# A decoder layer on one core: rows for the band mask, columns for the denominators, separate banks for maximum and exponential, and a pipeline of six steps over quads

## The reference

```
n = layernorm(x)
x = x + softmax(band(q k^T / sqrt(8))) v @ Wo      # self: query t sees keys t-63 .. t
n = layernorm(x)
x = x + softmax(q k^T / sqrt(8) - 100*mask) v @ Wo + bo   # cross: 77 tokens of ctx, with biases
n = layernorm(x); p = n shifted by one token
r = sigmoid((mu_r*n + (1-mu_r)*p) @ W_r^T); k = (mu_k*n + (1-mu_k)*p) @ W_k^T
x = x + r * (relu(k)^2 @ W_v^T)
```

## Time and profile before

| | |
|---|---|
| Runs | 1101.64 us (median of 3; 1100.23 to 1105.47) |
| Profiled execution | span 1103.0 us from first to last instruction; no other time of it is recorded |
| TensorE busy | 873.3 us (79%) |
| DVE, ACT, POOL busy | 681.8, 421.8, 194.1 us |
| Mean granted TensorE clock | 0.904 of full speed |
| DMA | 92.18 MB in 81317 packets; queue 1 busy 38.2% of 16 engines |

### The profile page before, as it was taken

One profiled execution on the slowest core, in us unless ns is written; L12 is line 12 of the kernel. 1 busy time (PEld: TensorE's weight loads), 2 busy tenths in 40 slices (PEclk: granted clock), 3 DMA queues, 4 the chain that ended last, 5 costly groups with the idle time before them and its releaser, 6 DMA issues.

```text
span 1103.0 us, 33918 instructions
## 1 busy us (share of the span) xinstructions
PE 873.3 (79%) x13841; PEld 613.2 (56%) x13967; DVE 681.8 (62%) x1540; ACT 421.8 (38%) x600; POOL 194.1 (18%) x176
## 2 busy tenths in 40 slices
...
GB/s 39 100 28 118 79 120 79 109 93 91 50 92 112 77 128 77 128 65 83 72 90 99 77 128 77 128 69 86 71 100 89 77 128 77 125 59 24 79 12 10
DMA packets 81317, 92.18 MB, mean 84 GB/s; under 512 B 14944, under 2 KB 75059, under 8 KB 76655
## 3 DMA queue, kind: packets, MB, share of 16 engines
q1 hardware_dynamic: 81262, 91.39, 38.2%
...
...
## 4 chain that ended last, share of the span: by engine, by line
PE 37%; DMA 26%; issue 12%; SPq 9%; ACT 7%; DVE 4%; POOL 4%; POOLq 0%; ACTq 0%; DVEq 0%
DMA q_stack<-q_scr 11%; DMA cq_stack<-cq_scr 9%; SPq L332 4%; PE score L975 4%; DMA q_scr<-q_parts 4%; PE score L1047 4%; PE sums L999 4%; PE score L971 4%; PE sums L1006 3%; PE score L986 3%; PE score L1063 2%; SPq L324 2%; PE score L1059 2%; ACT probs L539 2%; POOL cq_parts L455 2%
## 5 line engine op out<-in xcount | busy, mean ns | idle before, releaser
L548 ACT ACTIVATE cprobs<-score 77x1024 f32<-77x1024 f32 x128 | 129.6, 1013 | 234.6 <-PE score L1082 232.3
L539 ACT ACTIVATE probs<-score 128x1024 f32<-128x1024 f32 x128 | 129.4, 1023 | 135.8 <-PE score L1063 135.8
L813 DVE TENSOR_REDUCE cneg_max<-score 128x8 f32<-128x616 f32 x128 | 102.4, 800 | 77.8 <-PE score L1047 75.9
L798 DVE TENSOR_REDUCE neg_max<-score 128x8 f32<-128x1024 f32 x64 | 78.1, 1225 | 100.2 <-PE score L975 99.2
L971 PE MATMUL score<-band,pick_hi 128*128 128x512 bf16 x111 | 48.6, 520 | 61.3 <-DMA q_stack<-q_scr 59.5
L1047 PE MATMUL score<-ck_stack,cq_stack 99*128 99x77 bf16 x1024 | 60.7, 205 | 44.7 <-DMA cq_stack<-cq_scr 33.1
L1047 PEld LDWEIGHTS score<-ck_stack,cq_stack 99*128 99x128 bf16 x1024 | 47.0, 101 | 77.4 <-issue 34.6
L999 PE MATMUL sums<-cprobs,cv_heads 128*32 128x128 f32 x2048 | 82.9, 280 | 8.6 <-ACT cprobs L548 8.6
L447 POOL TENSOR_TENSOR rstd<-var_eps,neg_half 128x4 f32<-128x4 f32 x48 | 48.5, 1011 | 214.5 <-DVE var_eps L743 207.1
L1082 PE MATMUL score<-cq_stack,ck_stack 128*77 128x256 bf16 x512 | 78.2, 282 | 8.3 <-DMA cq_stack<-cmax_mid 8.3
L999 PE MATMUL sums<-probs,v_heads 128*32 128x128 f32 x2048 | 83.8, 282 | 0.0
...
## 6 DMA issues: line engine op xcount, KB each, us to landing
k_stack<-k_scr SPq DMA_DIRECT2D x32, 384.0 KB, 5.7
...
```

Source lines behind the costliest of these rows:

```text
L539: nc.scalar.activation(probs[:, k % 3].rearrange("p g a q -> p (g a q)"), score[ST_SLOT[k]][:, :], ACT.Exp).then_inc(exp_done, 1)
L548: nc.scalar.activation(cprobs[0:TC, k % 2].rearrange("p g a q -> p (g a q)"), score[k % 2][0:TC, :], ACT.Exp).then_inc(cexp_done, 1)
L813: nc.vector.tensor_reduce(cneg_max[:, a, :, b].rearrange("p (n i) -> p n i", n=2), src, AX_X, ALU.max, negate=True).then_inc(cmax_taken, 1)
```

## The change

All programs are rewritten. In parts:

1. **Stacks.** `q_stack` and `k_stack` hold one pair of sequences (p = 0 or 1) and one head in each column block: rows 0 to 63 are constants (an identity for the upper 64 queries, `key_mask` for the keys), rows 64 to 111 the 48 rows of parts, and 112, 113 the two maximum rows. Products for the upper queries use rows from 0 and get the band mask with them; those for the lower queries use rows from 64 and keep a mask product (`band_lo`, `band_loT`). `cq_stack` and `ck_stack` hold even pairs of heads in rows 0 to 52 and odd ones in rows 64 to 116, so a product spans half of the array's rows.
2. **Scores.** Turned self scores are computed without the quarter that the band hides: 16 products of 64 columns for the upper queries of one sequence, and 32 for the lower queries of two. There are 6 exponentials a quad for 8. Cross products are one head each.
3. **Denominators** are columns 16 and 17 of each head pair's 32 columns of `v_heads`, set to one. The sums are copied by ACT (`take_sums`), turned on TensorE (`turn_sums`), divided on DVE with tokens on partitions (`divide`), and turned back (`turn_att`): 24 more 128x128 turns a quad.
4. **Banks.** `score_max` serves only maxima and `score_exp` only exponentials, one tile of two banks each.
5. **Layer norms** go to POOL except for `bn_stats`: 9 small operations, a power, and two of 128x512. `x_step` replaces the two `mix_a`, `x1b` goes through DRAM and back, `x_res` is loaded again and not copied.
6. **Transfers** are by pair and by quad: 63 issues a quad. Parts are stored in pieces of 256 or 154 tokens.
7. **Pipeline.** `step(s)` works on quads s to s-5: 21 steps, of which s = 5 to 15 are full. q0: norm, q, k. q1: v, maxima, first half of the self attention. q2: second half, output, cross projections. q3: cross values, cross maxima, first half. q4: second half, output, norm. q5: feed forward.

The order on TensorE in a full step: last values of the first cross half (q4); `max_upper` q1; `scores_lower` q2; turns of q4; values q2; `max_upper`; `scores_upper` q2; feed forward products of q5 between `max_lower` q1 and more values; v of q1; four `cross_max` q3, three more and the first `cross_scores` of q4 with their values between them, with turns and projections of q2 and q0; then `scores_upper`, `scores_lower` q1; `max_upper`, `max_upper`, `max_lower` of q1's second pair, with projections of q2 and q4 between them; `cross_scores` and values of q3 between four `cross_max` of q3; turn of q4's norm; first `scores_upper` of q1's second pair.

```diff
-        q_stack = sb("q_stack", [P, 2, G, QB, T], BF16)
-        k_stack = sb("k_stack", [P, G, QB, T], BF16)
-        score = [stack.enter_context(nc.psum_tensor(f"score{n}", [P, 1024], F32)) for n in range(2)]
+        q_stack = sb("q_stack", [P, 2, 2, G, PB, T], BF16)
+        k_stack = sb("k_stack", [P, 2, 2, G, PB, T], BF16)
+        v_heads = sb("v_heads", [P, 2, QB, G, 32])
+        score_max = stack.enter_context(nc.psum_tensor("score_max", [P, 1024], F32))
+        score_exp = stack.enter_context(nc.psum_tensor("score_exp", [P, 1024], F32))
+        sums = [stack.enter_context(nc.psum_tensor(f"sums{n}", [P, PB, 2, T], F32)) for n in range(2)]
...
-                    for m in range(2):
-                        nc.tensor.matmul(dst[:, 512 * m:512 * m + 512], band[:, 0, :], ident_bf[:, :, :],
-                                         start=True, stop=False)
-                    for i in range(4):
-                        g = 2 * i + j
-                        last = nc.tensor.matmul(dst[:, 256 * i:256 * i + 256], k_stack[:, g, b, :],
-                                                q_stack[:, :, g, b, :], start=False, stop=(i % 2 == 1))
-                    last.then_inc(sT_made, 1)
...
+            def max_upper(q, p, b):
...
+                for g in range(G):
+                    for a in range(2):
+                        last = nc.tensor.matmul(score_max[HALF * a:HALF * a + HALF, T * g:T * g + T],
+                                                q_stack[0:ROW1, p, a, g, b, HALF:T], k_stack[0:ROW1, p, a, g, b, :],
+                                                start=True, stop=True)
+                last.then_inc(s_made, 1)
...
+            def max_lower(q, p):
+                for b in range(PB):
+                    nc.tensor.matmul(score_max[:, 512 * b:512 * b + 512], pick_lo[:, :, :], band_lo[:, :, :],
+                                     start=True, stop=False)
+                    for g in range(G):
+                        c = 512 * b + HALF * g
+                        for a in range(2):
+                            last = nc.tensor.matmul(score_max[HALF * a:HALF * a + HALF, c:c + HALF],
+                                                    q_stack[ROW0:ROW1, p, a, g, b, 0:HALF],
+                                                    k_stack[ROW0:ROW1, p, a, g, b, 0:HALF],
+                                                    start=False, stop=(g == G - 1))
+                last.then_inc(s_made, 1)
...
+            def scores_upper(q, p, b):
...
+                for a in range(2):
+                    for g in range(G):
+                        c = 512 * a + HALF * g
+                        last = nc.tensor.matmul(score_exp[:, c:c + HALF], k_stack[0:ROWS_SELF, p, a, g, b, :],
+                                                q_stack[0:ROWS_SELF, p, a, g, b, HALF:T], start=True, stop=True)
+                last.then_inc(sT_made, 1)
...
+            def scores_lower(q, p):
...
+                        for a in range(2):
+                            last = nc.tensor.matmul(score_exp[HALF * a:HALF * a + HALF, c:c + HALF],
+                                                    k_stack[ROW0:ROWS_SELF, p, a, g, b, 0:HALF],
+                                                    q_stack[ROW0:ROWS_SELF, p, a, g, b, 0:HALF],
+                                                    start=False, stop=(g == G - 1))
...
+            def upper(p, b, a, js=(0, 1)):
+                for j in js:
+                    for i in range(4):
+                        g = 2 * i + j
+                        c = 512 * a + HALF * g
+                        last = nc.tensor.matmul(sums[0][32 * i:32 * i + 32, b, a, HALF:T], v_heads[:, a, PB * p + b, g, :],
+                                                probs[:, 2 * b, c:c + HALF], start=(j == 0), stop=(j == 1),
+                                                tile_position=(0, 32 * i))
+                return last
...
+            def turn_four(dst, src):
+                for n in range(4):
+                    last = nc.tensor.transpose(dst[:, P * n:P * n + P], src(n), ident[:, :])
+                return last
+            def turn_sums(q, p, dst):
+                pe.wait_ge(raw_ready, 2 * q + p + 1)
+                turn_four(dst, lambda n: raw[:, n, :]).then_inc(raw_turned, 1)
...
+            def cross_max(q, p, b, a):
...
+                for i in range(4):
+                    for j in range(2):
+                        r, c = HALF * j, 512 * j + TC * i
+                        last = nc.tensor.matmul(score_max[:, c:c + TC], cq_stack[r:r + SHIFT_CROSS, p, i, a, b, :],
+                                                ck_stack[r:r + SHIFT_CROSS, p, i, a, b, :], start=True, stop=True)
+                last.then_inc(cs_made, 1)
...
+            def cross_scores(q, p, b, a):
...
+                for i in range(4):
+                    for j in range(2):
+                        r, c = HALF * j, 512 * j + T * i
+                        last = nc.tensor.matmul(score_exp[0:TC, c:c + T], ck_stack[r:r + ROWS_CROSS, p, i, a, b, :],
+                                                cq_stack[r:r + ROWS_CROSS, p, i, a, b, :], start=True, stop=True)
+                last.then_inc(csT_made, 1)
...
+            def divide(src, turned, inv, inv_ready, dst, ready, dst_turned, q, p):
...
+                heads = src[:, :].rearrange("p (n c) -> p n c", c=32)
+                nc.vector.reciprocal(inv[:, :, :], heads[:, :, 16:18]).then_inc(inv_ready, 1)
+                if later(q):
+                    dve.wait_ge(dst_turned, q)
+                dve.wait_ge(inv_ready, 2 * q + p + 1)
+                nc.vector.tensor_tensor(dst[:, p].rearrange("p b (n j d) -> p (b n) j d", j=2, d=DH),
+                                        heads[:, :, 0:16].rearrange("p n (j d) -> p n j d", j=2),
+                                        inv[:, :, :].unsqueeze(3).to_broadcast([P, 16, 2, DH]), ALU.mult)\
+                    .then_inc(ready, 1)
...
+            def moments_of(n, q):
+                pool.wait_ge(ln_stats[n], QB * q + QB)
+                if later(q):
+                    pool.wait_ge(ln_out[n], q)
+                mo, st = moments[n], stats[n]
+                nc.gpsimd.tensor_tensor(mo[:, 0], st[:, :, 1], st[:, :, 4], ALU.add).then_inc(ln_moments[n], 1)
+                nc.gpsimd.tensor_tensor(mo[:, 1], st[:, :, 1], st[:, :, 4], ALU.subtract).then_inc(ln_moments[n], 1)
+                nc.gpsimd.tensor_tensor(mo[:, 2], st[:, :, 2], st[:, :, 5], ALU.add).then_inc(ln_moments[n], 1)
+                pool.wait_ge(ln_moments[n], 7 * q + 3)
...
+                pool.wait_ge(ln_moments[n], 7 * q + 7)
+                nc.gpsimd.tensor_tensor(root[n][:, :], var_eps[n][:, :], neg_half[:, :], ALU.pow)\
+                    .then_inc(ln_root[n], 1)
+                pool.wait_ge(ln_root[n], q + 1)
+                nc.gpsimd.tensor_tensor(rstd[n][:, :], root[n][:, :], root[n][:, :], ALU.add).then_inc(ln_rstd[n], 1)
...
+            def norm_of(n, src, q, turned):
...
+                mean = moments[n][:, 3, :].unsqueeze(2).to_broadcast([P, QB, D])
+                nc.gpsimd.tensor_tensor(xn[n][:, :, :], src[:, :, :], mean, ALU.subtract).then_inc(ln_centred[n], 1)
+                pool.wait_ge(ln_rstd[n], q + 1)
+                pool.wait_ge(ln_centred[n], q + 1)
+                nc.gpsimd.tensor_tensor(xn[n][:, :, :], xn[n][:, :, :],
+                                        rstd[n][:, :].unsqueeze(2).to_broadcast([P, QB, D]), ALU.mult)\
+                    .then_inc(ln_out[n], 1)
...
+            def make_stack_rows():
+                dve.wait_ge(bands_made, 4)
+                nc.vector.tensor_copy(q_stack[0:HALF].rearrange("r p a g b t -> r (p a g b) t")[:, :, HALF:T],
+                                      ident[0:HALF, 0:HALF].unsqueeze(1).to_broadcast([HALF, 2 * H * PB, HALF]))\
+                    .then_inc(stack_rows, 1)
+                nc.vector.tensor_copy(k_stack[0:HALF].rearrange("r p a g b t -> r (p a g b) t"),
+                                      key_mask[:, :].unsqueeze(1).to_broadcast([HALF, 2 * H * PB, T]))\
+                    .then_inc(stack_rows, 1)
+                nc.vector.memset(k_stack[96:P].rearrange("r p a g b t -> r (p a g b t)"), 1.0)\
+                    .then_inc(stack_rows, 1)
...
+                for n, rows in enumerate((slice(32, 64), slice(96, 128))):
+                    nc.gpsimd.memset(cq_stack[rows].rearrange("r p i a b t -> r (p i a b t)"), 1.0)\
+                        .then_inc(cross_rows, 1)
+                    nc.gpsimd.memset(ck_stack[rows].rearrange("r p i a b t -> r (p i a b t)"), 1.0)\
+                        .then_inc(cross_rows, 1)
+                    pool.wait_ge(cross_rows, 2 * n + 2)
...
+            def store_self(parts, scr, lo, stored, q):
+                sp.wait_ge(lo, q + 1)
+                for p in range(2):
+                    sp.dma_start(scr[q][p].rearrange("c d n s -> (d n) c s"),
```

(70 more changed lines are left out.)

1890 lines of the change are left out of this document (1033 added, 857 removed).

## The result

The changed kernel takes 1021.54 us (median of 5, 1017.11 to 1037.98) against 1101.64 (5 runs, 1095.29 to 1109.53): a ratio of 0.924, 95% interval 0.918 to 0.931. It is faster, as forecast, but 113 us above the 908 and outside the range of 808 to 1010. The profiled execution is the slowest of the five (1037.98); where that matters the text goes by medians.

The account below looks back on a forecast made before the run. TensorE was taken as the bound, with some 11% of waits on top. Setup 83, early steps 155, 11 full steps of 47.5 and last steps 149 gave 910 us, 908 for the median; range 808 to 1010.

Parts of the forecast that it names:

- Together 4 us: a step of 47.5: Full steps: late shift rows and q4's norm add 4 us of waits to 43.5 us of TensorE work.
- The term of the shift rows: Waits in a step: shift rows of q3's first and q1's second pair each late by 0.5 to 1 us.
- rival 5: SP's in-order queue becomes the bound: a step of 66 us, 1113 us in all; chance 0.07.
- The shift rows of q4: Head of SP's step: issued behind other loads, they make q4's first cross scores wait about 1 us a step.
- TensorE's sum: TensorE's busy time over the program: from 873.3 to 696 us, 43.5 a quad; 569 to 820 by all ends.
- Self values: Self attention on TensorE: 2048 products of 64 columns at 49 ns, 100.5 us against 83.8, +16.7.
- rival 3: Short products on TensorE don't shrink: 5 to 7 us more a step, 990 us in all; chance 0.10.
- rival 2: TensorE packs better (row halves overlap, short products halve): 40 us a step with waits, 810 in all; chance 0.14.
- TensorE is the bound, with some 11% of waits on top: Kernel before: TensorE busy 873.3 of 1103.0 us, idle some 7 of 61.4 us a quad.
- the sum of -177: TensorE's terms added: -161.4 denominators, -48.6 mask, -32.6 self scores, +16.7 self values, -15 and -8 cross products, +72 turns.
- Rival 4: POOL's small norm operations cost as much as its power, 1.01 us and not 0.2: 990 us in all; chance 0.09.
- The ends: Setup and partial steps: 387 us, with the first stack landed at 83 after POOL's and DVE's fills in sequence.

Follow-up runs that it names:

- 0.30: The changed kernel without padding; the number is where its loop's first instruction stands in an estimated block of 256 TensorE instructions; 1021.54 us.
- 0.82: The changed kernel with 132 TensorE instructions of satisfied waits ahead of the loop, which puts its start at this fraction of a block; 944.60 us.
- 0.05: The changed kernel with 192 instructions of padding ahead of the loop, which puts its start at this fraction of a block; 1016.58 us.
- 0.75: The changed kernel with 114 instructions of padding ahead of the loop, which puts its start at this fraction of a block; 1008.71 us.
- the kernels with 43 and 58 packets: By instruction-queue packets: the kernel before, unpadded (43; 1101.64 us), and the changed kernel with 132 instructions of padding (58; 944.60 us).
- 0.55: The changed kernel with 64 instructions of padding ahead of the loop, which puts its start at this fraction of a block; 989.49 us.
- 1837 instructions with the same end: The kernel at 0.82 with three projections made twice and padding shortened so the loop ends at the same place; 1031.97 us.

## Why the prediction was wrong

**The step that failed is "Together 4 us: a step of 47.5".** Its list of waits had no place for TensorE's own instructions. The loop at 0.30 is fetched at each of its nine back edges, and the profiled steps are 56.3 us; at 0.82 the same kernel is fetched at one, has steps of 48.2 and takes 944.6. That is 77 us by the medians, two thirds of the 113, and the places 0.05 and 0.75 give it back. The two profiled executions, the slowest of the one kernel and the fastest of the other, lie 102 us apart: 56 of idle time, of which the gaps at these two lines are 51 (54.9 against 4.0), and 46 of busy time for the same 13999 records (782.1 against 736.0). The granted clock of the executions was 0.817 to 0.832, and 0.838 to 0.868 at 0.82. That the gaps lower the clock, and that this is the rest of the price, is argued from these rows, not isolated: at 0.82, too, the loop's first 16 products took 1.08 us at 528.74, after a wait of 1.35 us for the shift rows and without an edge gap.

The Trainium skill ("Runtime: NRT & Kernel Launch", "Instruction fetch mechanics") says that TensorE holds 2048 instructions, filled in blocks of 256 as a FIFO, and that a taken branch whose target is not in the current window of two blocks forces a fetch and stalls. The trace agrees with the stall, 3.3 us at the edge, and loops of 1807 and 1825 fit in 2048. It does not agree with a window of two blocks, nor with the same section's "there's no instruction cache that benefits from spatial locality": in the kernels with 43 and 58 packets the branch goes back over the whole loop, at ten of eleven and eight of nine edges, without a fetch.

**What remains of the 113.** The kernel at 0.82 has a span of 933.7 us against my 910: 8 of these 24 us are in the steps (48.2 for 47.5), 16 at the ends (403 for 387). Its median is 8 above the profiled execution.

**Which places are kept stays open.** At 0.82 the loop was fetched again at one, two or three of nine edges, and at one of eleven in the kernel before; at 0.05, 0.30, 0.55 and 0.75 it was fetched at every one. Counting blocks does not sort them, since at all five places the loop touches eight blocks, and 1837 instructions with the same end were not kept.

**The term of the shift rows was mis-sized**: 0.5 to 1 us for q1's second pair, measured 49.5 / 17 = 2.9, and 37.6 / 16 = 2.4 with the loop kept. I counted 2.4 us to issue these rows and too little for the six stores ahead of them (4.46 us) and the landing. But it was not free to take back: each of the four reorderings of SP's queue moved the wait to other rows, and all but the first were slower than what they started from. Of rival 5 that much is true: SP's order is tight. In the step from 565.35 us its issues add up to 37 us, for my 31, of 51.5. The shift rows of q4 were rated too high: they cost 3.9 us in the whole run.

**TensorE's sum: right by most of its parts, wrong as a reason.** Its busy sum is 736.0 with the loop at 0.82 and 782.1 as released, against 696 and within its 569 to 820 (added up again, the two ends are 571 and 816). Upper scores took 50.2 / 1024 = 49 ns for my 59, cross maxima 44 for 45, cross scores 58 for 68. Self values came to 58.8 + 44.2 = 103 us, for 100.5: short products do shrink, and rival 3 fell. Of rival 2, the row halves in alternation gained 3 to 5% only. Turns took 37.1 / 192 = 193 ns in L1130 and 24.7 / 128 = 193 in one group of L1278, for 173. Cross values were to keep their 83 and took 100.6, and 93.5 with the loop kept. But "TensorE is the bound, with some 11% of waits on top" was not so for the kernel before: with 81 us of its largest term left out it gains 9. Part of the 81 was never to be had, since the records that are left cost more; the other part came back as waits for hand-overs through DRAM, DVE and ACT. So that the sum of -177 led to nearly the right step is in part luck. The waits of the earlier trace rows, 92.6 us, are 29.1 after the change, so the new order, which loads each stack nearly a step ahead, may have earned what I credited to the products. No run tests the new order without the savings.

**Rival 4** fell: POOL's small operations took 203 ns (L513), as taken.

**The ends**: the first maximum product came at 58.5 us, not 83. I had put POOL's fills and DVE's stack rows one after the other, 22 + 17 us. They run beside each other, and the first stack waits for DVE's rows alone, which end at 48.2:
```profile
36.34 3.23 DVE L867 COPY k_stack<-key_mask 64x8192 bf16<-64x8192 bf16 x1
37.38 3.95 POOL L493 MEMSET v_heads<- 128x2048 f32 x1
41.27 1.80 POOL L493 MEMSET cv_heads<- 128x2048 f32 x1
41.34 6.88 DVE L870 MEMSET k_stack<- 32x8192 bf16 x1 [1.76 <-issue]
```
The rule that I had inferred holds for the copy and not for the fill. Beside DVE's copy (L867, to 39.57) POOL's fill took 3.95 us, 2.15 more than the equal one behind it; beside DVE's own fill (L870) POOL's took its plain 1.80. Besides, the fills of `cq_stack` were of 4096 columns, 3.5 us each, where I had counted 8192, and DVE's rows took 2.27 + 3.23 + 6.88 = 12.4 us, for 17.
```profile
58.48 1.07 PE L1185 MATMUL score_max<-k_stack,q_stack 112*64 112x128 bf16 x16 [25.81 <-DMA q_stack<-q_scr]
```
In spite of these 25 us all that is not a full step came to 416 instead of 387: the partial steps are hardly shorter than full ones. In the kept kernel the first intervals of `x1b` are 50.9 and 52.6 us, where I had 38 to 45 for such steps, since, as I read it, each already holds a whole chain of maxima, rows and exponentials.
